# Cross attention over the context in a two-layer kernel: 128-row query tiles, shares scaled on two engines and turned on VectorE, values in four row groups

## The reference, cut to what matters

```python
kv_rope = kv_c * cos[None] + _rotate_half(kv_c) * sin[None]
q_r = jnp.einsum('bshq,hqr->bhsr', q_big, W_qr)
k_r = jnp.einsum('bld,hdr->bhlr', kv_rope, W_kr)
scores = jnp.einsum('bhsr,bhlr->bhsl', q_r, k_r)
attn = jax.nn.softmax(scores, axis=-1)
ctx_c = jnp.einsum('bhsl,bld->bhsd', attn, kv_rope)
ctx_lat = jnp.einsum('bhsd,hkd->bshk', ctx_c, w_kc_kv)
out = ctx_lat.reshape(b, s, H * K) @ Wo.T
```

## Time and profile before

| | |
|---|---|
| median of 3 runs | 1620.16 us (1620.1 to 1620.33) |
| the profiled execution's own time | 1619.06 us |
| its span, first to last instruction | 1617.2 us |
| PE busy | 1576.2 us (97%) |
| DVE, ACT, POOL busy | 934.6, 732.1, 667.9 us |
| granted TensorE clock | full in all 40 slices of the span |
| the stage, from the second unit's scores to the first wait behind it | about 422 to 607 us |
| most that the DMA engines moved in one slice | 273 GB/s |

### The profile page before, as it was taken

One profiled execution on the slowest core, in us unless ns is written; L12 is line 12 of the kernel. 1 busy time (PEld: TensorE's weight loads), 2 busy tenths in 40 slices (PEclk: granted clock), 3 DMA queues, 4 the chain that ended last, 5 costly groups with the idle time before them and its releaser, 6 DMA issues.

```text
span 1617.2 us, 24572 instructions
## 1 busy us (share of the span) xinstructions
PE 1576.2 (97%) x9834; PEld 1344.5 (83%) x9834; DVE 934.6 (58%) x1525; ACT 732.1 (45%) x1231; POOL 667.9 (41%) x489
## 2 busy tenths in 40 slices
PE   9999999999999999999999989999999999999998
PEld 8997667788899998778889977777778788888887
DVE  7555663366544555587768657345766545554554
ACT  3114564322677765666611146334555333353342
POOL 2974542540498873331227634122424232222221
PEclk9999999999999999999999999999999999999999
DMA  5110003133222007200001100110011111111211
GB/s 170 65 62 19 2 2 130 45 103 127 90 82 66 14 1 273 69 1 1 27 14 66 53 27 1 51 52 21 15 34 52 46 52 60 51 40 46 65 47 46
DMA packets 28580, 88.52 MB, mean 55 GB/s; under 512 B 4154, under 2 KB 4282, under 8 KB 28215
## 3 DMA queue, kind: packets, MB, share of 16 engines
q1 hardware_dynamic: 28468, 86.96, 16.2%
HBM read 85.11 MB, written 1.84 MB: 54 GB/s over the span
## 4 chain that ended last, share of the span: by engine, by line
PE 85%; DVE 6%; ACT 4%; issue 4%; POOL 1%; DMA 0%; SPq 0%; ACTq 0%; DVEq 0%; POOLq 0%
PE PS L263 19%; PE PS L265 19%; PE PS L264 19%; PE PS L268 7%; PE PS L1165 5%; PE PS L1503 3%; PE PS L1520 2%; PE PS L600 2%; PE PS L624 1%; PE PS L992 1%; PE PS L1756 1%; PE PS L1744 1%; PE PS L590 1%; PE PS L608 1%; DVE Sb L1816 0%
## 5 line engine op out<-in xcount | busy, mean ns | idle before, releaser
L312 POOL TENSOR_TENSOR HL<-stg,HL 128x1024 fp32r<-128x1024 f32 (+2 forms) x109 | 238.5, 2190 | 497.7 <-ACT HL L307 479.6
L263 PE MATMUL PS<-XT,HL 128*128 128x448 f32 x608 | 224.0, 368 | 0.7 <-POOL HL L312 0.6
L264 PE MATMUL PS<-XT,HL 128*128 128x448 f32 x608 | 222.1, 365 | 0.0
L265 PE MATMUL PS<-XT,HL 128*128 128x448 f32 x608 | 222.1, 365 | 0.0
L307 ACT ACTIVATE HL<-stg 128x1024 fp32r<-128x1024 f32 (+2 forms) x110 | 103.6, 944 | 212.7 <-PE PS L265 197.2
L263 PE MATMUL PS<-HL,XT 128*128 128x512 f32 (+1 forms) x380 | 137.1, 361 | 0.8 <-DVE XT L764 0.8
L265 PE MATMUL PS<-HL,XT 128*128 128x512 f32 (+1 forms) x380 | 134.2, 353 | 0.0
L264 PE MATMUL PS<-HL,XT 128*128 128x512 f32 (+1 forms) x380 | 134.1, 353 | 0.0
L263 PEld LDWEIGHTS PS<-XT,HL 128*128 128x128 f32 x608 | 114.2, 188 | 12.5 <-POOL HL L312 1.0
L264 PEld LDWEIGHTS PS<-XT,HL 128*128 128x128 f32 x608 | 114.3, 188 | 9.0
L265 PEld LDWEIGHTS PS<-XT,HL 128*128 128x128 f32 x608 | 114.2, 188 | 9.1
(11 more groups left out here) (323 smaller groups left out, 3820.3 us busy)
## 6 DMA issues: line engine op xcount, KB each, us to landing
stg<-in_wst SPq DMA_DIRECT2D x87, 512.0 KB, 3.3
stg<-in_wst SPq DMA_DIRECT2D x16, 352.0 KB, 3.1
stg<-in_wst SPq DMA_DIRECT2D x16, 320.0 KB, 3.1
wsum<-in_wfc SPq DMA_DIRECT2D x8, 512.0 KB, 3.7
wsum<-in_wpj SPq DMA_DIRECT2D x8, 512.0 KB, 3.5
raw<-in_wfc SPq DMA_DIRECT2D x8, 512.0 KB, 6.5
stg<-in_wst SPq DMA_DIRECT2D x16, 256.0 KB, 2.7
raw<-in_wpj SPq DMA_DIRECT2D x7, 512.0 KB, 7.1
```

Source lines behind the costliest of these rows:

```text
L263: e.matmul(out, lh, rh, start=start, stop=False)
L264: e.matmul(out, lh, rl, start=False, stop=False)
L265: return e.matmul(out, ll, rh, start=False, stop=stop)
L312: e.tensor_tensor(slot(k)[:, 1, 0:n], stg[k % NSTG][:, 0:n], slot(k)[:, 0, 0:n].bitcast(F), A.subtract).then_inc(*done(*low_part(k)))
```

## The change

The stage is done in 16 halves of a batch. A half is eight heads, 896 query rows, cut into seven tiles of 128 rows. There are still 64 units, four to a half: three of two tiles and one of one tile (`tiles`). Query parts are made per half in two pieces of 512 and 384 columns. POOL scales the shares of three units of each half, and DVE those of the fourth. The shares are turned by DVE, in blocks of 32 x 32, from `Sx` to `TX` (rows padded from 375 to 384 columns by memsets). Because only blocks are turned, the rows 32r to 32r+31 of `TX` hold the context index within a block, for the queries 32r to 32r+31 of each tile: so the values are made in four row groups, each with its own PSUM bank (4 to 7), over 12 blocks of 32 context rows (`x_values`, 48 products of 224 columns per half, in three portions of four blocks). For this each batch's rotated context must lie four times over the partitions (`V4`): SP writes the rotated rows to DRAM (`rotated`) and reads each batch back four times (`replicate`). ACT copies the result of a half from the four banks to `QO` (`out`). The transposes of PE, the `PX` copies of ACT and the `QO` copies of DVE go away. `TX` takes the place of two `HL` slots, so only `ox` piece 0 is split during the stage; pieces 1 and 2 come at its end, and the loads of pieces 4 and 5 stand behind the magnitudes.

```diff
-    cut_no = {k: i for i, k in enumerate(cuts)}
+    cut_no = {k: i + (k >= piece["ox", 0][0]) for i, k in enumerate(cuts)}
+    cut_of = {i: k for k, i in cut_no.items()}
...
-        Sx = [at(f"Sx{i}", [S, 2, L], F, rSCR + i * 3008) for i in range(4)]
+        Sx = [at(f"Sx{i}", [128, 2, LP], F, rSCR + i * 8 * LP) for i in range(4)]
+        TX = [at(f"TX{i}", [128, 7, LP], F, (rHL, rSCR + 32 * LP)[i]) for i in range(2)]
+        V4 = [at(f"V4{i}", [128, LP // 32, 128], F, rKV + 12000 + i * 16 * LP) for i in range(2)]
+        rotated = nc.dram_tensor("rotated", (NB, LP, 128), F).ap()
...
+            if s:
+                e.wait_ge(*upon("pe_x", "sc", 4 * s - 3 + 2 * i))
...
         def pool_x(e):
             for st in range(UX + 1):
-                if st % 2 == 0 and st + 2 < UX:
-                    query_parts(e, st + 2)
+                if st % 4 == 0 and st < UX:
+                    query_parts(e, st // 4, 1)
+                if st % 4 == 2 and st + 2 < UX:
+                    query_parts(e, st // 4 + 1, 0)
                 if st % 8 == 4 and st // 8 + 1 < NB:
                     keys_parts(e, st // 8 + 1)
-                if st:
+                if st % 4:
                     u = st - 1
-                    k = u % 4
                     e.wait_ge(*upon("dve_x", "rx", u))
-                    e.tensor_tensor(Sx[k][:, :, :], Sx[k][:, :, :], rx[:, k, :].unsqueeze(2).to_broadcast([S, 2, L]),
-                                    A.mult).then_inc(*done("pool_x", "p", u))
-                if st in (6, 12, 18):
-                    rest_w(e, piece["ox", st // 6 - 1][0])
+                    x_share(e, u).then_inc(*done("pool_x", "p", u))
+                if st == 6:
+                    rest_w(e, piece["ox", 0][0])
+            for i in range(1, 3):
+                rest_w(e, piece["ox", i][0])
+
+        def x_share(e, u):
+            k, n = u % 4, len(tiles(u))
+            return e.tensor_tensor(Sx[k][:, 0:n, 0:L], Sx[k][:, 0:n, 0:L], rx[:, k, 0:n].unsqueeze(2).to_broadcast([P, n, L]), A.mult)
...
+            for t in tiles(u):
+                o = t % 4 * 128
+                last = mm3(e, PS[:, bank + t % 2, 0:L + 1], qxh[i][:, o:o + 128], qxl[i][:, o:o + 128], kxh[b % 2][:, :],
...
+        def x_values(e, s, j0, j1):
+            b = s // 2
+            if j0 == 0:
+                e.wait_ge(*upon("dve_x", "t", 4 * s + 3))
+                e.wait_ge(*upon(f"sp_v4{b % 2}", b, 3))
+                if s:
+                    e.wait_ge(*upon("act_x", "o", s - 1))
+                else:
+                    for half in range(2):
+                        e.wait_ge(*upon("dve_q", "o", 7, half))
+                        e.wait_ge(*upon("act_q", "o", 7, half))
+            for j in range(j0, j1):
+                for r in range(4):
+                    p = slice(32 * r, 32 * r + 32)
+                    last = e.matmul(PS[:, 4 + r, 0:224], V4[b % 2][p, j, :], TX[s % 2][p, :, 32 * j:32 * j + 32], start=j == 0,
+                                    stop=j == LP // 32 - 1)
+            if j1 == LP // 32:
+                last.then_inc(*done("pe_x", "pv", s))
 
         def pe_x(e):
...
             for st in range(UX + 4):
+                s, k = st // 4, st % 4
                 if 0 < st < UX:
                     x_scores(e, st)
-                if 0 <= st - 3 < UX:
-                    u = st - 3
-                    e.wait_ge(*upon("pool_x", "p", u))
-                    if u:
-                        e.wait_ge(*upon("act_x", "px", u - 1))
-                    else:
-                        e.wait_ge(*upon("act_q", "o", 7, 0))
-                        e.wait_ge(*upon("act_q", "o", 7, 1))
-                    for e_ in range(2):
-                        for c in range(3):
-                            last = tr(e, PS[0:125, 4 + e_, c * S:(c + 1) * S], Sx[u % 4][:, e_, c * 125:(c + 1) * 125], S)
-                    last.then_inc(*done("pe_x", "tr", u))
-                if 0 <= st - 4 < UX:
-                    u = st - 4
-                    e.wait_ge(*upon("act_x", "px", u))
-                    if u > 1:
-                        e.wait_ge(*upon("dve_x", "o", u - 2))
-                    else:
-                        e.wait_ge(*upon("pool_ctx", "k", NB - 1))
-                        e.wait_ge(*upon("dve_q", "o", 7, 1))
-                    for c in range(3):
-                        last = e.matmul(PS[:, 6 + u % 2, 0:2 * S], kvr[:, c, u // 8, :], PX[u % 2][:, :, c, :],
-                                        start=c == 0, stop=c == 2)
-                    last.then_inc(*done("pe_x", "pv", u))
+                if s > 1 and k < 2:
+                    x_values(e, s - 2, 4 + 4 * k, 8 + 4 * k)
+                if 0 < s <= UX // 4 and k == 3:
+                    x_values(e, s - 1, 0, 4 if s < UX // 4 else 12)
...
+            e.wait_ge(*upon("act_x", "exp", UX - 1))
+            value_of(e, 1)
+            e.wait_ge(*upon("act_mag", 15))
+            e.matmul(PS[:, 2, 0:16], C("ones"), gam[:, :, 8:16], start=True, stop=True).then_inc(*done("pe_thr"))
 
...
+            def out(s):
+                e.wait_ge(*upon("pe_x", "pv", s))
+                e.activation(slot_of(s).rearrange("p (t r q) -> p r t q", t=7, r=4),
+                             PS[:, 4:8, 0:224].rearrange("p r (t q) -> p r t q", t=7), ACT.Copy).then_inc(*done("act_x", "o", s))
...
-                if 0 <= st - 3 < UX:
-                    u = st - 3
-                    if u > 1:
-                        e.wait_ge(*upon("pe_x", "pv", u - 2))
-                    e.wait_ge(*upon("pe_x", "tr", u))
-                    e.activation(PX[u % 2][:, :, :, :].rearrange("p e c s -> p e (c s)"), PS[0:125, 4:6, 0:3 * S],
-                                 ACT.Copy).then_inc(*done("act_x", "px", u))
+                s, k = st // 4, st % 4
                 if st < UX:
-                    k, bank = st % 4, 2 * (st % 2)
+                    bank = 2 * (st % 2)
                     if st > 3:
-                        e.wait_ge(*upon("pe_x", "tr", st - 4))
+                        e.wait_ge(*upon("dve_x", "t", st - 4))
                     e.wait_ge(*upon("dve_x", "nm", st))
-                    for e_ in range(2):
-                        last = e.activation(Sx[k][:, e_, :], PS[0:S, bank + e_, 0:L], ACT.Exp, bias=nm[:, k, e_:e_ + 1],
-                                            scale=1.0, accum_out=sx[:, k, e_:e_ + 1])
+                    for i in range(len(tiles(st))):
+                        last = e.activation(Sx[k][:, i, 0:L], PS[:, bank + i, 0:L], ACT.Exp, bias=nm[:, k, i:i + 1], scale=1.0,
+                                            accum_out=sx[:, k, i:i + 1])
                     last.then_inc(*done("act_x", "exp", st))
-                if st in (4, 10, 16):
-                    round_w(e, piece["ox", st // 6][0])
+                if k == 2 and s > 1:
+                    out(s - 2)
+                if st == 4:
+                    round_w(e, piece["ox", 0][0])
...
-                if st in (52, 54, 56, 58):
-                    ox_hi(e, (st - 52) // 2, 0)
+                if st in (55, 57, 59, 61):
+                    ox_hi(e, (st - 55) // 2, 0)
                 if st == UX + 1:
                     value_hi(e, 0)
+            round_w(e, piece["ox", 1][0])
+            out(UX // 4 - 1)
+            round_w(e, piece["ox", 2][0])
...
         def dve_x(e):
-            for st in range(UX + 4):
+            for st in range(UX + 2):
                 if 0 < st < UX:
                     x_largest(e, st)
                 if 0 <= st - 1 < UX:
                     u = st - 1
-                    k = u % 4
+                    k, n = u % 4, len(tiles(u))
                     e.wait_ge(*upon("act_x", "exp", u))
-                    e.reciprocal(rx[:, k, :], sx[:, k, :]).then_inc(*done("dve_x", "rx", u))
-                if 0 <= st - 4 < UX:
-                    u = st - 4
-                    e.wait_ge(*upon("pe_x", "pv", u))
-                    e.tensor_copy(pair_of(u), PS[:, 6 + u % 2, 0:2 * S].rearrange("p (e s) -> p e s", e=2)).then_inc(*done("dve_x", "o", u))
-                if st in (53, 55, 57, 59):
-                    ox_lo(e, (st - 53) // 2, 0)
-                if st == UX + 2:
-                    value_lo(e, 0)
+                    e.reciprocal(rx[:, k, 0:n], sx[:, k, 0:n]).then_inc(*done("dve_x", "rx", u))
+                if st == 1:
+                    e.wait_ge(*upon("pool_ctx", "k", NB - 1))
+                    e.wait_ge(*upon("pe_q", "k", 7, 1, 1))
+                    for i in range(4):
+                        e.memset(Sx[i][:, :, L:LP], 0.0).then_inc(*done("dve_x", "pad", i))
+                if st > 1:
+                    u = st - 2
+                    s = u // 4
+                    if u % 4 == 0 and s > 1:
+                        e.wait_ge(*upon("pe_x", "pv", s - 2))
+                    if u % 4 == 3:
+                        e.wait_ge(*upon("dve_x", "rx", u))
+                        x_share(e, u).then_inc(*done("dve_x", "p", u))
```

(87 more changed lines are left out.)

32 lines of the change are left out of this document (13 added, 19 removed).

## The result

The change makes the kernel slower: 1663.6 us (1660.22 to 1663.7) against 1620.24 us (1620.1 to 1621.23) before. The ratio is 1.0263, with a 95% interval of 1.0251 to 1.0275. The prediction had the sign, but 1631.4 us was too low by 32 us, and the time lies outside the range.

The account below looks back on a forecast made before the run. A loop through PE's wait for ACT's copy was to bound the kernel: 13 halves +9.2, head -2, tail +4, together +11.2 us on 1619.06, 1630.3, plus 1.1 for the median: 1631.4 us; range 1616 to 1650.

Parts of the forecast that it names:

- PE's own sum: PE's work per half after the change: scores 3.57, values 4.6, six mode changes 1.14, together 9.3 us.
- rival 3: DVE's transposes cost more, 1.1 us each, or keep POOL from SBUF: half 12.6 to 13.4 us, 1639 to 1650; chance 0.13.
- A change of mode: PE switching between whole-array and row-group work, six times a half: a hole of 0.19 us each, 1.14 us together.
- rival 1: Mode changes on PE cost nothing, as the next weights load ahead: half 11.05 us, kernel 1619 us; chance 0.12.
- DVE beside POOL: DVE's share meets POOL's work in each half: 0.55 us added to POOL, making 9.4 us a half.
- The wait: PE's values wait once a half for ACT's copy out(s-2), issued behind unit 4s+2's exponentials: PE idle 2.9 us, half 12.0 us.
- Rival 2: The loop through ACT's copy doesn't bind and POOL sets 9.4 us a half: kernel 1598 us; chance 0.12.
- a half takes 12.0 us: Steady stretch, units 10 to 62: 12.0 against 11.28 us before, over 13 halves, +9.2 us.
- rival 4: PE waits 2.9 us each half and its clock falls; at half speed a half takes 20 us, kernel 1735; chance 0.03.
- The prediction's own sign of being wrong: Values portions over 1.7 us; also PE's idle ended by something else, or the second-token-tile product before 607.
- The head: Up to unit 10's scores: -2 us, with the context's copies through DRAM hidden; if not, up to 5 us.
- The tail: From unit 62's scores to the product with the second token tile: 18.1 us against 14.1 before, +4 us.

Follow-up runs that it names:

- the repaired kernel: The changed kernel with ACT's copy ahead of the exponentials and the rotated-context transfers ahead of the last two weight loads: 1604.1 us; the same kernel as e4.
- e1: The changed kernel with ACT's copy out(s-2) issued ahead of unit 4s+2's exponentials instead of behind them: 1612.77 us, ratio 0.9951 to the kernel before.
- e4: The changed kernel with both ACT's copy ahead of the exponentials and the rotated-context transfers earlier: 1604.1 us, ratio 0.9898 to the kernel before.
- e2: The changed kernel with 16 unused matmuls of 372 columns a half filling PE's idle time before the first values portion, the wait kept: 1641.56 us.
- e8: The changed kernel with 8 unused matmuls of 372 columns a half in PE's idle time instead of e2's 16, the wait kept: 1643.75 us.
- e3: The changed kernel with SP issuing rotated and the first two replicate ahead of the last two weight loads: 1655.65 us.
- e5: e2 with the values of a half in two portions of six blocks instead of three of four: 1658.98 us.
- e6: e4 with the values of a half in two portions of six blocks instead of three of four: 1623.3 us, ratio 1.0018 to the kernel before.

## Why the prediction was wrong

- **What bounds it.** PE sets the pace before, and in the repaired kernel again. PE's own sum of 9.3 us a half was nearly right: 47.79 of 50 us at a half of 9.94 us are 9.50 us.
- **The prices.** The portions of values: 32 instructions at full clock took 1.80 us and 96 took 4.82 us (at 642.80), so 1.51 us per 32, predicted 1.53. The transposes: 555 ns on average, 0.51 us each in pairs, predicted 0.5; rival 3 is out. The copy: 914 ns, predicted 0.90. A change of mode: 0.17 to 0.18 us, predicted 0.19; rival 1 is out. Here the Trainium skill's rule in "TensorEngine Tiling (Array Packing)", section Key Properties, that a change of mode drains the engine, has its price for this shape.
- **DVE beside POOL.** DVE's share at 505.63 (0.53 us) met POOL's share, which took 1.66 us where it takes 1.44 beside DVE's transposes (+0.22, predicted +0.55):

```profile
505.63 0.53 DVE L1133 TENSOR_TENSOR Sx<-Sx,rx 128x375 f32<-128x375 f32 x1
```

```profile
496.92 1.44 POOL L1133 TENSOR_TENSOR Sx<-Sx,rx 128x750 f32<-128x750 f32 x1
...
505.79 1.66 POOL L1133 TENSOR_TENSOR Sx<-Sx,rx 128x750 f32<-128x750 f32 x1 [5.92 <-DVE rx L1234]
```

- **The wait.** Mechanism, place and length were right. PE waits once a half for `out(s-2)`, 2.73 us, predicted 2.9; a half at full clock is 12.2 us, predicted 12.0. Rival 2 (the loop doesn't bind, 9.4 us, 1598) is what e1 and e4 make of the kernel, at 10.08 and 9.94 us: the loop hung on the written order on ACT, as the prediction said of it.
- **The step that failed: the clock.** The term "a half takes 12.0 us" was used for 13 halves, and the fall of the clock stood beside it as rival 4, as a matter of all or nothing: half speed throughout, 20 us a half, 1735, with a chance of 0.03. The runs show the case between. PE falls to 1.2 GHz behind its idle time and is back at 2.4 GHz with the next unit's scores: 1.58 us a half in all but the first of those told apart above. This makes 13.6 us a half on average, and +30.3 us where +9.2 was summed: +11.7 for the loop at full clock, +18.6 for the clock. e2 and e8 take 20 us back by filling the idle time alone. The prediction's own sign of being wrong, portions of over 1.7 us, came true here. The ground that I gave, that the trace of before shows no fall, was no evidence: before, PE has no idle time of this kind in the stage. The Trainium skill has the pattern, in "TensorE: Matmul & The Clock Gate", section HAM oscillation — how this bites in real kernels: waits between short bursts bring the slow clock back at each burst. The traces agree with this, at 13 of the 14 waits for the copy; but that section's waits are for transfers, of some 3 to 5 us, and here 2.73 us behind another engine did it.
- **The head.** Predicted -2 us, with "up to 5 us" if the copies weren't hidden; it was +7.3, of which 1.2 lay ahead of the stage. Two steps failed. The first is the rate: the writes were priced at the fastest slice's 273 GB/s, about 6 us, and between 416 and 430 us, while they ran, the DMA engines moved 108 to 113 GB/s (DMA share 0.36 to 0.39, where the reads back have 1.14 to 1.25), so that they took 17.1 us with their landing. The reads back ran at 190 to 231 GB/s (432 to 440 us). The second is the sentence that these instructions stand on no other engine's queue: they stand on SP's, ahead of the magnitudes, and ACT waits for these ahead of an exponential. With the transfers moved, e3 gives 8.0 us back, and its head is 2.0 us shorter than before (24.5 against 26.5), which is the predicted -2. Why the writes are slow is open. The rows of 512 bytes alone aren't it, since the reads have such rows too.
- **The tail.** Predicted +4, measured +5.5. The steps predicted are there: the values start 3.40 us after unit 62's scores (634.26 - 630.86, predicted 3.38), the copy, the last half's 96 instructions in 4.82 us, the copy and the rounding. What was missing is the clock again. The 64 instructions at 634.26 took 4.79 us, where at full clock, in e2 and e8, they took 3.31 us.

## What to carry to other kernels

An idle time of an engine that is near its bound costs its own length and, on TensorE, can cost the work behind it at half the clock as well: here 1.58 us behind 2.73 us. A trace that has no such idle time says nothing about that. A copy that frees a buffer belongs, in the written order, ahead of what it does not depend on: here one instruction moved was worth 51 us and turned a loss of 2.6% into a gain, and with the transfers moved too into a gain of 1.0%. What stands between two dependent steps may be their cover; before portions are merged or moved to save changes of mode at 0.17 us each, look at which chain runs beside them.

## What was not expected of the hardware

- The clock: behind 2.73 us without a matmul it fell to 0.50 for some 3.3 us, though not at the first wait shown (457.35). Behind 1.36 us (e8) and behind 1.41 us alone (e5, e6) it did not; behind 1.41 and 1.09 us with a tile between (e6) it did. What pattern brings it down is open beyond these. In the stretches shown it read 1.00 during the idle time and 0.50 once work was back.
- SP can stand in a transfer's issue for microseconds. Of the writes of `rotated` the first, of 500 KB, took 0.33 us to issue, the next two 4.18 and 4.19 us, and the last, of only 36 KB, 4.63 us; the reads back took 0.31 to 0.50 us each. So neither the size nor the rows of 512 bytes set this time by themselves. That SP stood behind the writes already under way fits, but isn't shown.
- 32 x 32 transposes of float32 on VectorE, 384 columns: 0.51 us each. Two shares on POOL beside them took 2.83 us, 1.42 each, as alone.
